# Another order of the DMA queue, and of three engines' work, in a linear-attention and FP6 feed-forward kernel

## The reference, cut to what matters

```python
x = x + _layernorm(_L0_attn_ref(_layernorm(x), Wq, bq, Wk, bk, Wv, bv, Wo, bo))
x = x + _layernorm(_L0_ffn_ref(_layernorm(x), weight, bias))

# _L0_attn_ref: x is (4, 4096, 512), 16 heads of 32
q = elu(x @ Wq.T + bq) + 1;  k = elu(x @ Wk.T + bk) + 1;  v = x @ Wv.T + bv
numerator   = einsum('bhtd,bhtde->bhte', q, cumsum(k v^T over t))
denominator = maximum(einsum('bhtd,bhtd->bht', q, cumsum(k over t)), 1e-6)
out = (numerator / denominator) @ Wo.T + bo

# _L0_ffn_ref: rows in blocks of 32, each rounded to an FP6 grid times its scale
out = dequantise(quantise(x)) @ dequantise(quantise(weight)).T + bias
```

## Time and profile before

| | us |
|---|---|
| median of 3 runs | 2397.83 (2393.44 to 2398.91) |
| the profiled execution's own time | 2399.21 |
| its span in the profile | 2397.4 |
| TensorE matmul busy | 2332.0 (97%) |
| VectorE busy | 1984.1 (83%) |
| GpSimd busy | 1470.3 (61%) |
| ScalarE busy | 1080.8 (45%) |
| mean DMA rate | 82 GB/s |

### The profile page before, as it was taken

How to read it: one execution, slowest core, us unless ns; L and a number is a source line. 1 busy time by engine, 2 the same in 40 slices (tenths; PEclk the granted TensorE clock), 3 DMA queues, 4 the chain that set the end, 5 groups by cost and what they waited for, 6 DMA issues and landing times.

```text
span 2397.4 us, 63827 instructions
## 1 busy us (share of the span) xinstructions
PE 2332.0 (97%) x26146; PEld 1905.0 (79%) x26146; DVE 1984.1 (83%) x3988; ACT 1080.8 (45%) x1840; POOL 1470.3 (61%) x1730
## 2 busy tenths in 40 slices
PE   7999999999999999999999999999999999999997
PEld 5877888888788788888787887888878888878785
DVE  7888889888788888898888887888988888878886
ACT  4444444444444444444444444444444444444442
POOL 2566566666566665666665665656666656656554
PEclk9999999999999999999999999999999999999999
DMA  4222221222222322222322222222123222223211
GB/s 158 71 92 98 75 77 62 88 99 73 86 65 75 99 90 80 77 65 86 99 73 90 73 71 91 96 76 75 62 89 99 73 90 73 71 91 95 77 46 37
DMA packets 108227, 195.55 MB, mean 82 GB/s; under 512 B 15136, under 2 KB 21664, under 8 KB 107424
## 3 DMA queue, kind: packets, MB, share of 16 engines
q1 hardware_dynamic: 107936, 191.47, 24.5%
HBM read 155.65 MB, written 35.78 MB: 80 GB/s over the span
## 4 chain that ended last, share of the span: by engine, by line
PE 79%; DMA 7%; DVE 4%; ACT 3%; issue 3%; POOL 2%; SPq 2%; POOLq 0%; DVEq 0%; ACTq 0%
PE work L423 12%; PE work L425 11%; PE work L424 11%; PE score L423 10%; PE score L424 10%; PE score L425 10%; PE work L540 5%; PE work L442 4%; PE score L505 4%; DMA rden_dram<-rinv 3%; DMA kc<-rden_dram 3%; PE state_bank L553 1%; POOL f_buf L1425 1%; DVE A L1020 1%; PE score L527 1%
## 5 line engine op out<-in xcount | busy, mean ns | idle before, releaser
L1020 DVE TENSOR_TENSOR A<-score,causal 128x512 f32<-128x512 f32 x512 | 329.2, 681 | 21.5 <-PE score L505 21.5
L1395 POOL TENSOR_TENSOR exp_t<-exp_t,x_coef 128x512 f32<-128x512 f32 x124 | 198.5, 1601 | 148.6 <-DMA exp_t<-in_xt 148.6
L725 ACT CAST oT_hi<-kc 128x512 fp32r<-128x512 f32 x128 | 79.6, 622 | 365.4 <-DVE kc L1015 365.4
L1402 POOL TENSOR_TENSOR x_res<-x_res,o_buf 128x512 f32<-128x512 f32 x128 | 175.6, 1372 | 104.5 <-ACT o_buf L670 104.5
L423 PE MATMUL work<-wo_hi,oT_hi 128*128 128x512 f32 x512 | 204.2, 399 | 14.8 <-ACT Kn L720 11.9
L423 PE MATMUL work<-wv_hi,xT_hi 128*128 128x512 f32 x512 | 214.9, 420 | 0.0
L423 PE MATMUL score<-xT_hi,wq_hi 128*128 128x512 f32 x512 | 208.1, 406 | 6.8 <-DVE KT L960 6.8
L1397 POOL TENSOR_TENSOR exp_t<-exp_t,x_coef 128x512 f32<-128x512 f32 x124 | 205.2, 1655 | 9.7
L423 PE MATMUL score<-xT_hi,wk_hi 128*128 128x512 f32 x512 | 205.7, 402 | 0.0
L425 PE MATMUL work<-wv_hi,xT_lo 128*128 128x512 f32 x512 | 202.2, 395 | 0.6 <-issue 0.6
L424 PE MATMUL work<-wv_lo,xT_hi 128*128 128x512 f32 x512 | 201.8, 394 | 0.9 <-issue 0.9
(11 more groups left out here) (134 smaller groups left out, 6393.1 us busy)
## 6 DMA issues: line engine op xcount, KB each, us to landing
x_in<-in_x SPq DMA_DIRECT2D x128, 256.0 KB, 4.3
x_res<-in_x SPq DMA_DIRECT2D x128, 256.0 KB, 2.8
kc<-rden_dram SPq DMA_DIRECT2D x128, 256.0 KB
exp_t<-in_xt SPq DMA_DIRECT2D x124, 256.0 KB, 3.1
out<-f_buf SPq DMA_DIRECT2D x96, 256.0 KB, 2.0
x_coef<-coef_dram SPq DMA_DIRECT2D x31, 512.0 KB, 3.8
out<-xd SPq DMA_DIRECT2D x32, 256.0 KB, 2.1
rden_dram<-rinv SPq DMA_DIRECT2D x32, 64.0 KB, 3.5
```

What stands on the lines that cost most here:

```text
L1020: nc.vector.tensor_tensor(A[:, j, :, :], score_bank[j][:], causal[:].unsqueeze(1).to_broadcast([P, G, P]), ALU.mult).then_inc(a_set, 1)
L1395: nc.gpsimd.tensor_tensor(rows, rows, by_token(0), ALU.mult).then_inc(x_scaled, 1)
L1402: nc.gpsimd.tensor_tensor(x_res[:, b, :], x_res[:, b, :], o_buf[:, b % 2, :], ALU.add).then_inc(r_set, 1)
```

## The change

SyncE's order is written anew: reciprocals go ahead of x by features, residual rows go towards the end, and x by rows is loaded for tile i+2 in place of i+1 (tile 1's is loaded before the first turn). The orders of ScalarE, VectorE and GpSimd are changed too. No instruction is added or taken away inside a full turn, and TensorE's order stays. SyncE's part whole, and of the others the parts that the text speaks of:

```diff
             def turn(i, prev, cur, nxt):
-                if nxt:
-                    load_x(i + 1, 0)
-                    load_x(i + 1, 1)
-                    load_x(i + 1, 2)
-                    load_x(i + 1, 3)
+                after = i + 2 < TILES
                 if prev:
                     store(i - 1, 0)
-                if cur:
-                    load_res(i, 0)
+                if after:
+                    load_x(i + 2, 0)
+                    load_x(i + 2, 1)
                 if nxt:
                     store_coef(i + 1)
                     spread_coef(i + 1)
                 if prev:
                     store(i - 1, 1)
-                if cur:
-                    load_res(i, 1)
-                if nxt:
-                    load_xt(i + 1, 0)
-                    load_xt(i + 1, 1)
+                if after:
+                    load_x(i + 2, 2)
                 if cur:
                     store_rden(i)
                     spread_rden(i, 0)
+                if nxt:
+                    load_xt(i + 1, 0)
+                if cur:
                     spread_rden(i, 1)
-                    spread_rden(i, 2)
-                    spread_rden(i, 3)
+                if nxt:
+                    load_xt(i + 1, 1)
                 if prev:
                     store(i - 1, 2)
                 if cur:
-                    load_res(i, 2)
+                    spread_rden(i, 2)
+                    load_res(i, 0)
                 if nxt:
                     load_xt(i + 1, 2)
+                if cur:
+                    spread_rden(i, 3)
+                if nxt:
                     load_xt(i + 1, 3)
                 if prev:
                     store(i - 1, 3)
+                if after:
+                    load_x(i + 2, 3)
                 if cur:
+                    load_res(i, 1)
+                    load_res(i, 2)
                     load_res(i, 3)
...
+            for b in range(NSEQ):
+                load_x(1, b)
             turn(0, False, True, True)
```

ScalarE, the middle of a turn:

```diff
                 for j in range(HPG):
                     past(j)
+                kn(0)
                 seed(0)
-                kn(0)
+                kn(1)
                 o_hi(0)
-                seed(1)
                 if nxt:
                     x_hi(i + 1, 0)
                 f_norm(2)
-                kn(1)
+                seed(1)
+                seed(2)
                 if nxt:
                     x_hi(i + 1, 1)
                 o_hi(1)
                 o_norm(i, 0)
```

VectorE, around the reciprocals and at the end of a turn:

```diff
                 xd_lo(3)
-                f_seen(2)
                 clamp()
                 invert()
-                join(i - 1, "f", 2)
+                f_bias(2)
+                f_seen(2)
                 v_bias(0)
                 mask(0, 0)
...
                 f_bias(3)
                 normalise(0)
+                mask(1, 0)
+                f_seen(3)
+                mask(1, 1)
                 o_lo(0)
-                f_seen(3)
-                mask(1, 0)
-                mask(1, 1)
-                join(i - 1, "f", 3)
+                if nxt:
+                    x_lo(i + 1, 0)
                 v_bias(1)
...
                 greatest(i, 0)
                 scale(i, 0)
                 if nxt:
+                    x_lo(i + 1, 2)
+                quantise(i, 0)
+                if nxt:
                     x_lo(i + 1, 3)
-                quantise(i, 0)
+                o_bias(i, 2)
                 normalise(3)
-                o_bias(i, 2)
+                o_seen(i, 2)
+                o_lo(3)
                 r_seen(i, 1)
-                o_lo(3)
                 join(i, "r", 1)
                 widen(i, "r", 1)
-                o_seen(i, 2)
                 join(i, "o", 2)
                 widen(i, "o", 2)
```

GpSimd, the middle of a turn:

```diff
                 rstd(i - 1, "f", 0)
                 dequantise(i - 1, 2)
+                output(0)
                 if nxt:
                     rstd(i + 1, "x", 2)
-                output(0)
+                product(0)
                 dequantise(i - 1, 3)
-                product(0)
                 product(1)
                 if nxt:
                     rstd(i + 1, "x", 3)
                 rstd(i - 1, "f", 1)
                 output(1)
+                rstd(i - 1, "f", 2)
                 if nxt:
                     x_scale(i + 1, 0)
-                rstd(i - 1, "f", 2)
+                output(2)
                 if nxt:
                     x_scale(i + 1, 1)
-                output(2)
                 rstd(i - 1, "f", 3)
                 rstd(i, "o", 0)
                 residual(i, 0)
```

More of the change, by code:

```diff
@@ L1236, in turn @@
                 join(i - 1, "o", 3)
-                scan(0)
+                r_seen(i - 1, 2)
                 widen(i - 1, "o", 3)
                 phi_k(1)
-                r_seen(i - 1, 2)
+                scan(0)
+                phi_k(2)
                 scan(1)
                 f_bias(0)
-                phi_k(2)
-                if nxt:
-                    widen(i + 1, "x", 1)
                 join(i - 1, "r", 2)
+                f_seen(0)
                 widen(i - 1, "r", 2)
                 r_seen(i - 1, 3)
-                if nxt:
-                    x_seen(i + 1, 3)
@@ L1251, in turn @@
-                xd_lo(1)
                 join(i - 1, "r", 3)
-                f_seen(0)
-                widen(i - 1, "r", 3)
-                greatest(i - 1, 2)
                 scan(2)
                 join(i - 1, "f", 0)
+                greatest(i - 1, 2)
+                widen(i - 1, "r", 3)
+                scale(i - 1, 2)
                 widen(i - 1, "f", 0)
-                scale(i - 1, 2)
+                xd_lo(1)
                 quantise(i - 1, 2)
+                phi_k(3)
                 if nxt:
-                    widen(i + 1, "x", 2)
+                    join(i + 1, "x", 2)
+                    x_seen(i + 1, 3)
@@ L1263, in turn @@
                 greatest(i - 1, 3)
                 scale(i - 1, 3)
-                phi_k(3)
+                f_bias(1)
                 scan(3)
-                quantise(i - 1, 3)
-                phi_q(0)
-                xd_lo(2)
-                phi_q(1)
                 if nxt:
                     join(i + 1, "x", 3)
-                f_bias(1)
-                f_seen(1)
-                phi_q(2)
+                    widen(i + 1, "x", 2)
+                quantise(i - 1, 3)
                 if nxt:
@@ L1277, in turn @@
                     widen(i + 1, "x", 3)
+                phi_q(0)
+                phi_q(1)
+                xd_lo(2)
+                phi_q(2)
+                product(2)
+                phi_q(3)
+                f_seen(1)
                 join(i - 1, "f", 1)
-                phi_q(3)
-                product(2)
                 widen(i - 1, "f", 1)
                 product(3)
-                f_bias(2)
                 xd_lo(3)
-                f_seen(2)
                 clamp()
                 invert()
-                join(i - 1, "f", 2)
+                f_bias(2)
@@ L1318, in turn @@
                 mask(2, 2)
+                v_bias(2)
                 mask(2, 3)
-                v_bias(2)
                 r_seen(i, 0)
                 o_bias(i, 1)
+                o_seen(i, 1)
                 join(i, "r", 0)
-                o_seen(i, 1)
+                widen(i, "r", 0)
                 normalise(2)
-                join(i, "o", 1)
                 mask(3, 0)
                 mask(3, 1)
-                widen(i, "r", 0)
+                mask(3, 2)
                 o_lo(2)
-                mask(3, 2)
-                if nxt:
-                    x_lo(i + 1, 2)
+                join(i, "o", 1)
                 mask(3, 3)
+                v_bias(3)
                 widen(i, "o", 1)
-                v_bias(3)
                 greatest(i, 0)
@@ L1438, in turn @@
                     rstd(i, "o", 0)
+                    residual(i, 0)
                     x_scale(i + 1, 2)
[L1440 to L1441 removed]
                     rstd(i, "r", 0)
                     rstd(i, "o", 1)
+                    x_scale(i + 1, 3)
                     dequantise(i, 0)
@@ L1466, in turn @@
                     return
+                residual(i - 1, 2)
+                if nxt:
+                    rstd(i + 1, "x", 0)
                 dequantise(i - 1, 1)
-                residual(i - 1, 2)
                 rstd(i - 1, "o", 3)
                 residual(i - 1, 3)
-                if nxt:
-                    rstd(i + 1, "x", 0)
                 rstd(i - 1, "r", 2)
```

43 lines of the change are left out of this document (19 added, 24 removed).

## The result

The changed kernel takes 2469.19 us (median of 4 runs, 2462.32 to 2477.58) where the kernel before takes 2397.15 (4 runs on the same chip, 2393.44 to 2398.91): a ratio of 1.0304, 95% interval 1.027 to 1.0339, so **72 us slower**. I had forecast +7. The profiled execution took 2462.32, the fastest of the four and 63.1 above that of before, so the trace can account for 63 of the 72.

A forecast was written before the change was run, and what follows sets the result against it. TensorE, busy 97% of the span, was taken as the bound, leaving only its losses between matmuls, 52.7 us. Terms -22.4 + 32.5 + 3 - 6 = +7 on 2397.8 gave 2405 us; forecast's own range 2400 to 2416, 8-in-10 range 2376 to 2420.

The forecast's parts named there:

- Residual rows: End of the turn: load_res(i,1), moved late, makes xd_transposes(0) wait 1.05 us in each of 31 turns, +32.5 us.
- x by features: load_xt(0) behind the reciprocals' store lands at about 46.1 instead of 42.6; GpSimd's later work 0.4 us later a turn.
- ScalarE's and VectorE's other moves: Other reorderings on these two engines keep at least 0.5 us of slack, covered by TensorE's own work: 0.
- Reciprocals: Before o(i,0) and attend(1): their earlier store removes normalise(0)'s DMA wait, -22.4 us, bounds -23.4 and -12.
- lock: Rival, before o(i,0): o_lo(0) meets an x_scale half in most turns, ends 0.5 late; +15, 2420 us, chance 0.10.
- x by rows and the irregular issues: SyncE's queue: x by rows two tiles ahead wins nothing; irregular issues ahead of load_res(i,1) cost +3 us, bounds 0 and 9.
- Instruction gaps: TensorE, transposes to v(0): coefficients' broadcast about 0.85 us later holds up other instruction fetches; -6 us, bounds -22 and +12.
- `x_lo(3)` behind two others: Before k(0): x_lo(3) behind x_lo(2) and quantise(0) waits 0.3 to 0.5 us, hidden by the transposes' wait; alone about 10.
- The landing by the Trainium skill: Residual load of 256 KB: about 2.0 us fixed plus bytes over 436 GB/s, estimated 2.6; +20 in place of +32.5.
- the trace's blame on `Kn`: Before o(i,0): the trace names ScalarE's Kn for the gap; the prediction blamed o_lo(0) and the reciprocals, 23.4 us with attend(1).

The follow-up runs named there:

- e3: The changed kernel with load_res(i,1) moved ahead of store(i-1,2): 2442.12 us, ratio 1.0192 to the kernel before.
- e6: The kernel before with store_rden alone moved ahead of load_xt(0) and load_xt(1), the reciprocals' loads staying behind them: 2373.95 us, ratio 0.9919.
- e13: e2 with store_rden alone moved ahead of load_xt(0) and load_xt(1), as in e6: 2385.76 us, ratio 0.9966 to the kernel before.
- e4: The changed kernel with ScalarE's kn(2) moved ahead of o_norm(i,0): 2475.64 us, ratio 1.034 to the kernel before.
- e7: The changed kernel with load_xt(0) and load_xt(1) put back ahead of store_rden: 2427.67 us, ratio 1.0144 to the kernel before.
- e2: The changed kernel with SyncE's whole order of the kernel before, so only the other engines' orders are new: 2416.62 us, ratio 1.0086 to the kernel before.
- e8: The changed kernel with both the edits of e3 and e7: 2410.29 us, ratio 1.0075 to the kernel before.
- e9: e6 with the 512 KB broadcast of coefficients moved right behind store_rden, ahead of x by features: 2416.49 us, ratio 1.0083 to the kernel before.
- e10: As e9, but with the broadcast of coefficients behind load_xt(0), load_xt(1) and the first reciprocals' load: 2539.67 us, ratio 1.0586 to the kernel before.
- e5: The kernel before with ScalarE's kn(1) moved ahead of o_hi(0): 2395.68 us, ratio 1.0008.
- e12: e9 with ScalarE's kn(1) moved ahead of o_hi(0), as in e5: 2398.2 us, ratio 0.9999 to the kernel before.
- e1: The kernel before with the changed kernel's SyncE order alone, other engines as before: 2562.52 us, ratio 1.0695.
- e11: e2 with VectorE's stretch from normalise(0) to normalise(1) in the order of the kernel before: 2413.64 us, ratio 1.0065 to the kernel before.

## Why the prediction was wrong in size and right in sign

The sign held, and so did the residual rows' wait, which I had said decides; but I had given "slower" only 0.50, and most of the 72 us comes from a place that I had priced at nothing, so the sign is partly luck. Of the signs that I had named, those of being right came (GpSimd's wait for the DMA into `x_res`, the gap at `xd_transposes(0)`), and one of being wrong too: the gap at `o(i,0)` stayed. The range (2376 to 2420) missed by 49 us. By steps:

- *Residual rows, "+32.5".* Right: +32.8 in the trace, 26 us of time given back by e3. Its make-up differs. `residual(i,1)` has the wait of 2.15 for the DMA, but nearly half is lost already before `o(i-1,3)`, since `o_lo(3)` meets the late `residual(1)`: it took over 1.0 us in 23 of 30 turns (1.54 in turn 16), and 0.68 in all 30 before.
- *x by features, "all that follows on GpSimd is 0.4 later. Bounds 0 and 0.9".* **This step failed.** From `o(i,0)` to the end of `rstd(o,0)` it was 1.66 later (6.46 to 8.12), and `o(i,0)` itself came 0.4 later in the turn (51.91 to 52.31, medians). The landing and `x_scale(0)` were counted nearly right (-4.0 ahead of `o(i,0)`, counted -4.4); what I missed is that `shift_o` then falls on VectorE's `o_lo(1)` and `x_lo`. It took over 0.8 us in 27 of 30 turns, and 0.27 in all 30 before. I had priced the landing of the load but nothing that its delay runs into. At three places together it is up to 59 us: 27 before `o(i,1)`, 11 before `o(i,0)` and 21 before `attend(1)`.
- *ScalarE's and VectorE's other moves, "keep at least 0.5 us of slack ... 0".* Failed with it. The slack was there, but too small for a chain that is 1.66 later: `kn(2)` ends 9.44 behind `o(i,0)` (7.81 before), where `o(i,1)` starts at 8.47 in e6 and e13. It is 27 us in the trace. `x_lo(0)` ahead of two masks had no slack either: it waits in 13 turns. e4 adds that the term shouldn't be priced at the gate of `o(i,1)`: GpSimd's chain is late, and any gate on it shows it. e7 prices the order of the loads: 38 us, although in e7 the reciprocals are late again and cost 10 more than in after. It is the largest term of the change, where mine was 0.4 a turn inside another term.
- *Reciprocals, "-22.4".* Failed in this kernel, sound as a mechanism. The place lost 12.2 instead of winning 22.4. The store left later and landed later than I took (medians 0.47 and 2.92, taken 0 and 2.6), so the "DMA wait is gone" in only 10 of 30 turns; e13 shows that this did little harm. `o_lo(0)` was to start at 49.3 into the turn and end at 50.0; in turn 16 it starts at 50.46, of which 0.95 is the wait at `xd_transposes(0)` that lies before it, and ends at 51.94, kept by the half of `x_scale(0)` that ends at 51.40. That is the rival *lock*, which "would have to end after 49.9"; I gave it 0.10 and +15. It came in 16 of 30 turns and cost 11. The other 21, before `attend(1)`, I had nowhere. Early reciprocals with an early x by features win what I had counted: e6, -19.4 us, and e13, -31 against e2.
- *x by rows and the irregular issues, "+3".* Not seen: the rest of the queue makes no difference clear of noise (e8 against e2).
- *Instruction gaps, "-6".* -11.4, inside the bounds. e9 and e10 show the broadcast's part: moving it away halves them. The other half is there without it.
- *`x_lo(3)` behind two others.* Counted as 0 here and about 10 alone; ahead of `k(0)` it is 1.2 us in the kernel after and 5.7 in e2 and e13.
- *The landing by the Trainium skill (DMA: Bandwidth & Descriptors, on the two cost components), an estimated 2.6.* Too short: the residual row took 3.24 (median) from issue to use. The section's fit is of DMAs issued by GpSimd, and these are SyncE's.
- *That the trace's blame on `Kn` is not the cause.* Right for before (e5), and not in general (e12).

What I missed in common to all this: I let the load by features wait behind the store's landing and checked one deadline, that of its first reader. Its readers' readers, up to a PSUM buffer freed on ScalarE and a port shared with VectorE, had less slack than the 0.4 to 1.7 us that it used. And I read the deadlines in one turn, the one without gaps; the landing of the store alone varies from 2.4 to 4.6 us between turns.

## What to carry to other kernels

On a queue that issues in order, a store that is ready goes first, and the loads that need its landing go behind independent loads: the same store moved by itself won 19 us, and with the waiting load right behind it, ahead of the loads by features, it cost 38 (e7 against the kernel after). When a load is made later, follow the delay through every engine to the last buffer it frees, and look which long operation of another engine each step then falls on. An operation that waits for another engine belongs behind those that don't need it: `o_lo(3)` behind `r_seen(1)` cost 84 us in e1, `x_lo(0)` ahead of two masks 21 in the kernel after. Before paying for the removal of a gap, ask whether the loop runs through the instruction named there: three gaps (e4, e5, e11) went away and their time came back a few steps later.
